# Last stage of a graph and expert kernel: normalised rows kept in PSUM, first pairs on VectorE, one more load

## The reference, cut

```python
def reference(x, src, dst, ...):
    x = x + gnn(layernorm(x), edge_index, ...)          # 6250 nodes of 256 features
    x = x + ffn(layernorm(x)[None], ...)[0]
    return x

def ffn(x, gate_w, gate_b, w1, b1, w2, b2, gamma, beta):
    topk_vals, topk_idx = top_k(x @ gate_w + gate_b, 2)
    topk_w = softmax(topk_vals)
    h = relu(x @ w1[e] + b1[e])                          # for each expert e
    expert_out = h @ w2[e] + b2[e]
    y = x + sum(topk_w * expert_out[topk_idx])
    return (y - mean(y)) / sqrt(var(y) + 1e-5) * gamma + beta
```

## Time and profile before

| | us |
|---|---|
| median of three runs | 3192.68 |
| the three runs | 3191.4, 3208.37, 3192.68 |
| the profiled execution, its own time | 3186.81 |
| its span | 3185.1 |
| start of stage 7 in the span | 3110.88 |

### The profile page before, as it was taken

One profiled execution on the slowest core, in us unless ns is written; L12 is line 12 of the kernel. 1 busy time (PEld: TensorE's weight loads), 2 busy tenths in 40 slices (PEclk: granted clock), 3 DMA queues, 4 the chain that ended last, 5 costly groups with the idle time before them and its releaser, 6 DMA issues. The chain is left out here.

```text
span 3185.1 us, 43688 instructions
## 1 busy us (share of the span) xinstructions
PE 1771.6 (56%) x9011; PEld 1444.0 (45%) x9012; DVE 1754.0 (55%) x4247; ACT 1115.8 (35%) x2079; POOL 1871.5 (59%) x1936
## 2 busy tenths in 40 slices
PE   6343545455454545445454545554454555899994
PEld 5232434343343434334343434343343434799993
DVE  6544546455554646555554645455564645665655
ACT  3323333333333333333333333342333332343433
POOL 2356666666666666666666666666666651555555
PEclk9667777776777777777777778777777767999997
DMA  5433344443434344343434444343443436433336
GB/s 189 114 114 111 108 127 122 111 125 109 127 110 128 107 125 126 110 127 107 125 110 124 122 113 124 110 125 107 129 123 110 125 97 207 127 106 99 107 104 247
DMA packets 185080, 393.00 MB, mean 123 GB/s; under 512 B 50833, under 2 KB 107626, under 8 KB 178772
## 3 DMA queue, kind: packets, MB, share of 16 engines
q0 software_dynamic: 90864, 262.34, 29.1%
q1 hardware_dynamic: 77524, 115.84, 11.8%
q10 hardware_dynamic: 16656, 14.43, 2.0%
HBM read 355.94 MB, written 36.52 MB: 123 GB/s over the span
## 5 line engine op out<-in xcount | busy, mean ns | idle before, releaser
L1267 POOL DMA_INDIRECT gat<-table,idx x1627 | 1546.8, 951 | 905.1 <-issue 471.7
L1366 PE MATMUL ps_sum<-msg,hot 128*128 128x264 f32 x3322 | 1097.6, 502 | 709.7 <-DVE msg L1413 449.1
L1366 PEld LDWEIGHTS ps_sum<-msg,hot 128*128 128x128 f32 x3322 | 829.7, 256 | 920.3 <-issue 726.3
L1413 DVE TENSOR_TENSOR msg<-gat,ps_weight 128x2304 f32<-128x2304 f32 x196 | 472.0, 2408 | 564.3 <-ACT ps_weight L1324 359.0
L1279 ACT ACTIVATE hotT<-dst_row,neg_id 128x4352 bf16<-128x4352 int16 x48 | 188.2, 3921 | 518.0 <-DMA dst_row<-dst_half 485.4
L1352 PE MATMUL ps_look<-dst_split,hotT 128*128 (+1 forms) x1661 | 80.8, 191 | 500.2 <-ACT hotT L1281 368.3
L1352 PEld LDWEIGHTS ps_look<-dst_split,hotT 128*128 128x128 bf16 x1661 | 67.2, 101 | 517.8 <-issue 489.3
L1566 DVE TENSOR_TENSOR num<-acc,ps_sum 128x264 f32<-128x264 f32 x49 | 21.0, 429 | 438.7 <-remote 241.9
L1410 DVE TENSOR_TENSOR hot<-ps_own,rel 128x1152 f32<-128x1152 f32 x196 | 250.2, 1277 | 0.0
L1324 ACT ACTIVATE ps_weight<-score 128x72 f32<-128x72 f32 x196 | 44.1, 225 | 508.7 <-DVE score L1404 494.8
L2130 PE MATMUL ps_ht<-xT,w_t 128*128 128x128 f32 x1712 | 214.5, 280 | 0.0
(11 more groups left out here) (412 smaller groups left out, 2135.4 us busy)
## 6 DMA issues: line engine op xcount, KB each, us to landing
dst_row<-dst_half SPq DMA_DIRECT2D x49, 1088.0 KB
gat<-table,idx POOLq DMA_INDIRECT x1661
b_t<-in_L_ffn_b_dram ACTq DMA_DIRECT2D x107, 128.0 KB
listing<-list_f SPq DMA_DIRECT2D x736, 0.5 KB
table<-rows SPq DMA_DIRECT2D x49, 128.0 KB, 1.7
y_rows<-y SPq DMA_DIRECT2D x48, 128.0 KB
x_all<-in_x_dram SPq DMA_DIRECT2D x6, 896.0 KB, 8.8
back<-chosen SPq DMA_DIRECT2D x3, 1792.0 KB, 17.6
```

The costliest lines, as they stand in the source:

```text
L1267: pool.indirect_dma_start(gat[:, GSTART[g] + k, :], None, table, bass.IndirectOffsetOnAxis(ap=idx[g][:, k:k + 1], axis=0)).then_inc(landed ...
L1366: made = pe.matmul(ps_sum[:, 0:SUM], hot[:, m, k, :], msg[:, m, k, :], start=(g == 0 and k == 0), stop=(g == NG - 1 and k == n - 1))
L1413: dve.tensor_tensor(msg[:, m, 0:n, 0:D].rearrange("p j (h d) -> p j h d", d=HD), gat[:, j:j + n, 0:D].rearrange("p j (h d) -> p j h d", d=HD),
```

## The change

`ScalarE` writes the normalised rows to a new PSUM tile `ps_norm` (one copy), and `lift` reads them there and writes `normed` in SBUF. The wait for `closed`, which kept ScalarE from a copy of `normed` that is still read, moves to VectorE's `lift`. `ps_pair` shrinks to four rows, and `mean_var` becomes an SBUF tile of its own, `mean_var7`. The pairs of group 0 are added by VectorE in one tensor_tensor in place in `back`; TensorE has none of group 0. The others are shared out as before. Groups 4 and 5 have a load each.

```diff
-        LOADS = ((0, 1), (1, 2), (2, 3), (3, 4), (4, 6), (6, 7), (7, 9))
-        LOAD_OF = (0, 1, 2, 3, 4, 4, 5, 6, 6)
-        ON_POOL = (0, 2, 3, 3, 3, 3, 3, 2, 0)
+        LOADS = ((0, 1), (1, 2), (2, 3), (3, 4), (4, 5), (5, 6), (6, 7), (7, 9))
+        LOAD_OF = (0, 1, 2, 3, 4, 5, 6, 7, 7)
+        ON_PE = (0, 3, 4, 4, 4, 4, 4, 2, 2)
...
-        ps_pair = [ctx.enter_context(nc.psum_tensor(f"ps_pair{b}", [P, MOST + 1, D], F32)) for b in range(2)]
+        mean_var = sb("mean_var7", [P, 2, MOST, 2])
+        ps_pair = [ctx.enter_context(nc.psum_tensor(f"ps_pair{b}", [P, max(ON_PE), D], F32)) for b in range(2)]
+        ps_norm = ctx.enter_context(nc.psum_tensor("ps_norm", [P, MOST + 1, D], F32))
...
             def norm(g):
                 act.wait_ge(scale_ready, g + 1)
-                if g >= 4:
-                    act.wait_ge(closed, g - 3)
                 for k in range(SIZE[g]):
                     rows = rows_in(AT[g] + k)
-                    act.activation(normed[0:rows, g % 4, k, :], row_sum(g, k, rows), ACT.Identity,
+                    act.activation(ps_norm[0:rows, k, :], row_sum(g, k, rows), ACT.Identity,
...
             def sums(g):
+                if g == 0:
+                    dve.wait_ge(came[LOAD_OF[0]], 16)
+                    link(dve.tensor_tensor(back[:, 0:AT[1], 0, :], back[:, 0:AT[1], 0, :], back[:, 0:AT[1], 1, :], ALU.add))
...
-                    last = dve.bn_aggr(mean_var(g)[:, k, :], stats[:, k, :])
+                    last = dve.bn_aggr(mean_var[:, g % 2, k, :], stats[:, k, :])
                 link(last)
-                dve.tensor_scalar(var_g[:, 0:SIZE[g]], mean_var(g)[:, :, 1], EPS, None, ALU.add).then_inc(stats_read, 1)
+                dve.tensor_scalar(var_g[:, 0:SIZE[g]], mean_var[:, g % 2, 0:SIZE[g], 1], EPS, None, ALU.add).then_inc(stats_read, 1)
...
-                dve.scalar_tensor_tensor(nmr_g[:, 0:SIZE[g]], mean_var(g)[:, :, 0], -1.0, rstd_g[:, 0:SIZE[g]],
+                dve.scalar_tensor_tensor(nmr_g[:, 0:SIZE[g]], mean_var[:, g % 2, 0:SIZE[g], 0], -1.0, rstd_g[:, 0:SIZE[g]],
                                          ALU.mult, ALU.mult).then_inc(scale_ready, 1)
...
                 dve.wait_ge(norm_ready, AT[g + 1])
-                lifting = dve.tensor_tensor(normed[:, g % 4, 0:SIZE[g], :], normed[:, g % 4, 0:SIZE[g], :], spread_tiles(gam[:, :], SIZE[g]), ALU.mult)
+                if g >= 4:
+                    dve.wait_ge(closed, g - 3)
+                lifting = dve.tensor_tensor(normed[:, g % 4, 0:SIZE[g], :], ps_norm[:, 0:SIZE[g], :], spread_tiles(gam[:, :], SIZE[g]), ALU.mult)
```

More of the change, by code:

```diff
@@ L2248, in stage7 @@
         block = ctx.enter_context(nc.Block(no_gpsimd_drain=True))
-        ON_PE = [SIZE[g] - ON_POOL[g] for g in range(GROUPS7)]
         PE_AT = [sum(ON_PE[:g]) for g in range(GROUPS7 + 1)]
-        def mean_var(g):
-            return ps_pair[g % 2][:, MOST, 0:2 * SIZE[g]].rearrange("p (k c) -> p k c", c=2)
         def rows_in(t):
@@ L2308, in _ @@
             for g in range(GROUPS7):
-                if ON_POOL[g]:
+                if g >= 1 and ON_PE[g] < SIZE[g]:
                     pairs(g)
@@ L2345, in sums @@
                         dve.wait_ge(paired, PE_AT[g] + min(k // 2 * 2 + 2, ON_PE[g]))
-                    else:
-                        dve.wait_ge(pooled, sum(1 for n in ON_POOL[:g + 1] if n))
+                    elif g >= 1:
+                        dve.wait_ge(pooled, sum(1 for h in range(1, g + 1) if ON_PE[h] < SIZE[h]))
                     dve.bn_stats(stats[0:rows, k, :], row_sum(g, k, rows)).then_inc(stats_read, 1)
```

## The result

The changed kernel takes 3215.06 us (median of 17 runs, 3205.8 to 3229.32) against 3202.95 us for the kernel before in the same 17 rounds (3191.4 to 3213.66). The ratio, taken over the rounds, is 1.0046, with a 95% interval of 1.0031 to 1.0062: it is slower, by 0.46% or 14.7 us. (The two medians by themselves lie 12.1 us apart.) That is clear of noise and just under the 0.5% that the prediction drew as its line.

What follows compares the result with a forecast made beforehand. The prediction saw stage 7 bound by a DMA until 3139.56, then by VectorE and ScalarE in turn, 5.8 us a group. Held nmr_g moved its end from 3179.77 to 3202.3, +22.5 us: median 3192.7 to 3215, range 3186 to 3220.

Steps and rivals of the forecast that it cites:

- The bound and the cycle: Stage 7: VectorE and ScalarE alternate; after the change 11.3 us a group with the pair sum, 9.6 without.
- `nmr_g` shut out: Stage 7, each group: nmr_g, now with two SBUF inputs, waits for GpSimd's closing add, 4.01 us, GpSimd 0.07 us ahead.
- The row that spoke against the lock: Stage 1, L450: an nmr of the same form took 0.17 us beside GpSimd; said to hardly decide.
- the lock: A VectorE instruction with two SBUF inputs and a GpSimd tensor_tensor shut each other out for whole instructions.
- The pair sum that stands behind it keeps the lock: Behind the closing add: GpSimd's ready pair sum also goes before nmr_g, 1.72 us more, up to 5.7 a group.
- The sum: Stage 7, times at which each group's nmr_g is ready: end at 3202.3 instead of 3179.77, 22.5 us slower.
- rival 1: Stage 7: GpSimd gets the lock but its next pair sum does not keep it; +14.4 us, median 3207, chance 0.17.
- `var_g`: Stage 7, SBUF to SBUF: can be shut out, but costs 0 where nmr_g has already waited for GpSimd.
- rival 2: Stage 7: nmr_g gets the port first and var_g is shut out; -2 us, or -8 without kept pair sums; chance 0.20.
- Product from PSUM: Stage 7 gamma product: leaves the lock and takes 2.02 us; 3.0 us come back at 3159.89, 0.9 at 3177.44.
- Group 0 and the cold TensorE: Start of stage 7: group 0 gains 3 us, but cold TensorE, first pair 3.82 us, makes group 1 2.4 us late.
- Split load: Groups 4 and 5: group 4 would land 4.7 us earlier, at 3134.8, but hidden since T(3), nmr_g of group 3, is at 3152.8.

Runs made afterwards that it cites:

- x4_only_mean_sbuf: The kernel before, with mean_var in SBUF and nothing else of the change; ratio to before 1.0054, stage 7 91.6 us.
- x3_rstd_psum: The kernel after, with a second reciprocal into a PSUM row that nmr_g reads instead of the SBUF one; stage 7 67.5 us, one execution.
- x1_late_close: The kernel after, with GpSimd's closing add of group g waiting for nmr_g of group g+1; ratio to before 0.9983, stage 7 70.0 us.
- x8_close_by_recip: The kernel after, with GpSimd's closing add of group g released by the reciprocal of group g+1; stage 7 68.4 us, one execution.
- after_again: The kernel after, unchanged, profiled again on the second chip of the experiments; ratio to before 1.0046, stage 7 87.3 us.
- after_third: The kernel after, unchanged, profiled a third time, on another chip; stage 7 91.0 us, one execution.
- x2_no_var: The kernel with the late closing add, without VectorE's var_g: ScalarE takes the root with eps as bias; 2751.42 us against 2759.12, ratio 0.9969.
- x7_pe_group0: The kernel without var_g and with the late closing add, group 0's pairs on TensorE again; ratio to before 0.998, stage 7 64.6 us.

## Why the prediction was right, point by point

- **The bound and the cycle: right.** VectorE and ScalarE in turn set the pace. The cycle with the pair sum was predicted at 11.3 and is 11.4 us (product to product, 3159.09 to 3170.46), the one without at 9.6 and is 9.5 (3190.86 to 3200.37).
- **`nmr_g` shut out: right**, and it makes the whole loss (x4_only_mean_sbuf). GpSimd's lead, 0.07 us in the forecast, was 0.02 to 0.07, and it decided in all eight groups. The two conditions, both inputs in SBUF and GpSimd first, are each shown by taking one away (x3_rstd_psum, x1_late_close, x8_close_by_recip). The row that spoke against the lock, L450 in the earlier trace rows, did not decide, as the prediction held.
- **"The pair sum that stands behind it keeps the lock": mis-sized.** The sum took it for five groups, 8.1 us. In group 1 the pair sum of group 3 began 0.14 us behind the closing add's end (3148.18 and 3148.04), late enough for `nmr_g` to have gone; in after_again and after_third the row of that pair sum names the load as what it waited for. `nmr_g` of group 1 was ready 19.2 us into the stage where the sum has 21.2. In the other four groups it was kept 2, 0 and 2 times in three executions. That is nearly all of the difference between the +22.5 of the sum and the +16.4, +13.1 and +16.8 that stage 7 shows. The truth lies between the forecast and rival 1 (+14.4), and the 14.7 us of the ratio is at rival 1. One row, 5.02 us, could show that a ready instruction **can** keep the port, not that it always does, and the product at 3153.91 of the same trace, 2.21 us, had shown that it need not. The prediction used the pair sum behind it, 3.60 us, for the lock in the other direction and did not see that it speaks for rival 1.
- **`var_g`: right in the steady groups** (0.17 in groups 2 to 8), missed in group 1, where it met the pair sum of group 2 and took 0.89 us in place of 0.17. It was the next thing to be late wherever `nmr_g` was freed, as rival 2 had it.
- **Product from PSUM: right in size** (2.02 for seven tiles, 0.69 for two), the same fixed time as from SBUF. Activations into PSUM: 3.37 for seven against 3.40; the bound of 0.3 was ten times too wide.
- **Group 0 and the cold TensorE: right.** First pair 3.78 us (3137.81 to 3141.59) where 3.82 was said. The granted clock was 0.50 in it (1.2 GHz), and TensorE had stood idle for 15.97 us; from 3147 to 3152 it was 1.00. Group 1's statistics began 12.7 us into the stage where the sum has 13.5, because it took the start of GpSimd's pair sum for the landing, and TensorE starts on the same load 1.0 us earlier (3137.81 and 3138.80).
- **Split load: right, as far as shown.** Group 4's `nmr_g` comes at 47.7 us into the stage, where even the shared load had landed 28.6 us into it before, so it should give nothing in the kernel after; no run has the kernel after with the shared load. Alone it gives 3.1.
- **The absolute time: luck.** 3215 was named and 3215.06 measured, but the kernel before had 3202.95 over 17 runs, not the 3192.68 of its first three. The forecast had a change that was 8 us too large (10 by the medians) and a start that was 10 us too low.

## What to carry to other kernels

Where GpSimd streams SBUF beside VectorE, the small instructions matter as much as the large: 7 numbers a partition waited 5.8 us because both inputs lay in SBUF. Keep one operand of each such instruction in PSUM, or give ScalarE its work, and release GpSimd behind the last small instruction and not ahead of it. When an operand is moved from PSUM to SBUF to make room, look up every reader of it, not only the one for whom the room was made.

## What the runs showed of the hardware that was not expected

- The order of two starts decides down to 0.02 us: GpSimd ahead by 0.02 held `nmr_g` for 2.33 us, VectorE ahead by 0.05 made it 0.17.
- Whether a GpSimd instruction that is ready behind another keeps the port from a waiting VectorE instruction differs between executions of one program, 4 of 12 in the kernel after, for reasons that these runs don't show. Over all profiles here it did so for 6 of 16 `nmr_g`, 1 of 7 gamma products and none of 9 `var_g`.
- The duration of a VectorE row that had to wait follows one formula to about 0.02 us, for instructions of 7 and of 1792 elements, a tensor_tensor, scalar_tensor_tensor or tensor_scalar: GpSimd's end - own start - 0.15 + own time.
- The kernel before took 2761 us on one chip and 3184 us on another, while the kernel after had a stage 7 of 91.0 and 87.3 us there, a difference of 3.7 us that two kept pair sums of 1.8 us explain. A gain in this stage is therefore worth another ratio on each chip: x2_no_var gained 7.7 us of 2759, x7_pe_group0 6.4 us of 3184.
